# Feed-forward of a decoder layer: second h value in front of the chain of scales, and each half of h's turned codes waited for by itself

## The reference

```python
def bit_linear(x, w):            # activations: 8-bit codes per row, weights: -1, 0, 1
    qx = activation_quant(x)     # s = 127 / max(max|x|, 1e-5); clip(round(x * s), -128, 127) / s
    qw = weight_quant(w)         # s = 1 / mean|w|; clip(round(w * s), -1, 1) / s
    return qx @ qw.T

x = layernorm(x2)                                    # rows of 512
h = silu(bit_linear(x, w_gate)) * bit_linear(x, w_up)   # rows of 2048
h = ln_weight * (h * rsqrt(mean(h * h) + 1e-6))
y = x2 + bit_linear(h, w_down)                       # rows of 512
```

## Time and profile before

| | |
|---|---|
| runs | 803.2 us median of 3 (801.63 to 804.7) |
| profiled execution | 803.17 us, of which 801.3 us are the span from the first to the last instruction |
| PE busy over the span | 734.9 us (92%) |
| DVE busy | 595.3 us (74%) |
| ACT busy | 471.8 us (59%) |
| POOL busy | 332.9 us (42%) |
| feed-forward | first h at 603.4 us, last h at 783.0 us |
| mean granted clock of TensorE | 0.982 |

### The profile page before, as it was taken

The page is one execution under the profiler, slowest core; times in us unless marked ns, Lnnn a source line. Parts: engine busy times, 40 slices in busy tenths (PEclk is TensorE's granted clock), DMA queues, the critical chain, the costliest instruction groups (busy, mean ns, idle before and its releaser), DMA issues. The chain is left out here.

```text
span 801.3 us, 14101 instructions
## 1 busy us (share of the span) xinstructions
PE 734.9 (92%) x5113; PEld 507.1 (63%) x5130; DVE 595.3 (74%) x1102; ACT 471.8 (59%) x1024; POOL 332.9 (42%) x330
## 2 busy tenths in 40 slices
PE   6988999999999999999887879999978999999995
PEld 4766777777777777777654568888853443343442
DVE  6886766877668866676567557788857999999974
ACT  4555667666667665767545224444426676677663
POOL 2011214223042133534475154445525577677563
PEclk9999999999999999999989989999998999999999
DMA  9300021314032141305330175445221233343232
GB/s 314 107 1 28 27 85 49 106 40 146 28 106 70 64 151 35 106 28 187 104 106 1 53 284 199 172 184 211 92 63 60 52 93 93 80 102 82 61 71 66
DMA packets 55218, 78.33 MB, mean 98 GB/s; under 512 B 36335, under 2 KB 38383, under 8 KB 53424
## 3 DMA queue, kind: packets, MB, share of 16 engines
q1 hardware_dynamic: 46336, 51.99, 21.1%
q0 software_dynamic: 8528, 24.93, 9.0%
q10 hardware_dynamic: 288, 0.52, 0.2%
HBM read 56.92 MB, written 17.59 MB: 93 GB/s over the span
## 5 line engine op out<-in xcount | busy, mean ns | idle before, releaser
L557 ACT ACTIVATE probs<-s_ps,neg_max 128x512 f32<-128x512 f32 (+2 forms) x256 | 152.3, 610 | 19.2 <-DVE neg_max L726 17.7
L726 DVE TENSOR_REDUCE neg_max<-s_ps 128x2 f32<-128x1024 f32 (+2 forms) x128 | 124.6, 1015 | 34.2 <-PE s_ps L964 33.7
L984 PE MATMUL pT_ps<-ident,probs 128*128 128x128 f32 x832 | 114.8, 279 | 10.1 <-DVE probs L747 9.1
L569 ACT ACTIVATE probs<-pT_ps 128x512 f32<-128x512 f32 x96 | 57.4, 598 | 102.3 <-PE pT_ps L984 101.5
L984 PEld LDWEIGHTS pT_ps<-ident,probs 128*128 128x128 f32 x832 | 93.6, 143 | 25.2 <-DVE probs L747 11.7
L747 DVE COPY probs<-pT_ps 128x512 f32<-128x512 f32 x112 | 76.7, 684 | 36.8 <-PE pT_ps L984 36.0
L1669 POOL TENSOR_TENSOR xg_own<-h,ln_w_sb 128x512 f32<-128x512 f32 x64 | 83.2, 1309 | 39.6 <-DVE h L1757 35.1
L1848 PE MATMUL gate_ps<-w_tern,xqT_home 128*128 128x512 bf16 x252 | 67.6, 391 | 15.6 <-DVE h L1757 12.0
L897 PE MATMUL side_ps<-w_hi 128*128 128x512 f32 x172 | 71.0, 413 | 0.0
L420 POOL TENSOR_TENSOR aT_hi<-norm,one_col 128x512 fp32r<-128x512 f32 x15 | 15.6, 1040 | 125.9 <-DVE norm L738 87.7
L1848 PE MATMUL up_ps<-w_tern,xqT_home 128*128 128x512 bf16 x254 | 67.5, 388 | 0.1
(11 more groups left out here) (276 smaller groups left out, 1677.6 us busy)
## 6 DMA issues: line engine op xcount, KB each, us to landing
w_piece<-w_ffn SPq DMA_DIRECT2D x24, 512.0 KB
w_stage<-w_ffn SPq DMA_DIRECT2D x12, 1024.0 KB
xres<-x POOLq DMA_DIRECT2D x4, 1024.0 KB, 5.7
xn<-x SPq DMA_DIRECT2D x3, 1024.0 KB
x<-xres POOLq DMA_DIRECT2D x3, 1024.0 KB, 4.8
xn<-c SPq DMA_DIRECT2D x2, 1024.0 KB, 5.0
v_next<-c SPq DMA_DIRECT2D x2, 1024.0 KB, 8.0
xn<-x SPq DMA_DIRECT2D x4, 256.0 KB, 3.3
```

What stands on the lines that cost most here:

```text
L557: nc.scalar.activation(weights[qt][:, h, at:at + width(qt)], s_ps[:, h, 0:width(qt)], ACT.Exp, bias=neg_max[:, qt % 2, h:h + 1], accum_out ...
L569: nc.scalar.activation(out, turned_p, ACT.Identity).then_inc(slot_copied[0], 1)
L726: nc.vector.tensor_reduce(neg_max[:, qt % 2, 2 * s:2 * s + 2], s_ps[:, 2 * s:2 * s + 2, 0:width(qt)], AX.X, ALU.max, negate=True).then_inc ...
L984: last = nc.tensor.transpose(pT_ps[:, k % 2, h * P:h * P + P], weights[qt][:, h, a:z], ident[:])
```

## The change

Three edits.

1. `mean_of` computes the same product of `bn_mv`, -1 and `rstd` as a `tensor_scalar` with `rstd` as its pointer scalar, in place of a `scalar_tensor_tensor` with `rstd` as its second tensor.
2. On VectorE `hidden(t, 1)` moves from behind `quantize_h(t - 1)` to in front of `scale_x`, behind `top_of_x`.
3. `h_turned` becomes two semaphores, one for each half. `pack(t, n)` waits only for half n of tile t - 1, and `down(t, g)` only for half g // 2 of tile t.

```diff
     def mean_of(self, dve, t):
         i = t % 2
         dve.wait_ge(self.rstd_ready, t + 1)
-        self.nc.vector.scalar_tensor_tensor(self.mean_rstd[:, i:i + 1], self.bn_mv[:, i, 0:1], -1.0, self.rstd[:, i:i + 1],
-                                            ALU.mult, ALU.mult).then_inc(self.mean_ready, 1)
+        self.nc.vector.tensor_scalar(self.mean_rstd[:, i:i + 1], self.bn_mv[:, i, 0:1], self.rstd[:, i:i + 1], -1.0,
+                                     ALU.mult, ALU.mult).then_inc(self.mean_ready, 1)
...
-        hq_packed, h_turned = sem("hq_packed"), sem("h_turned")
+        hq_packed, h_turned = sem("hq_packed"), [sem("h_turned0"), sem("h_turned1")]
...
                         sp.dma_start_transpose(hqT[:, t % 2, n * FK // HALVES:(n + 1) * FK // HALVES, :],
-                                               hq[:, n * HALF:n * HALF + HALF]).then_inc(h_turned, 16)
+                                               hq[:, n * HALF:n * HALF + HALF]).then_inc(h_turned[n], 16)
...
                     if inside(t - 1):
-                        act.wait_ge(h_turned, t * HALVES * 16)
+                        act.wait_ge(h_turned[n], t * 16)
...
                     if inside(t + 2):
                         front.top_of_x(dve, t + 2)
+                    hidden(t, 1)
+                    if inside(t + 2):
                         front.scale_x(dve, t + 2)
                     if inside(t - 1):
                         scale_h(t - 1)
                         quantize_h(t - 1)
-                    hidden(t, 1)
                     hidden(t, 2)
...
-                        pe.wait_ge(h_turned, (t + 1) * HALVES * 16)
+                        pe.wait_ge(h_turned[g // HALVES], (t + 1) * 16)
```

## The result

| | before | changed |
|---|---|---|
| median | 803.11 us (801.63 to 804.7, 13 runs) | 809.19 us (806.01 to 812.71, 13 runs) |
| span of the profiled execution | 801.3 us | 808.3 us |

The ratio is 1.0076, with a 95% interval of 1.006 to 1.0092: slower by 6.1 us, where 6.0 were forecast.

The account below looks back on a forecast made before the run. The prediction took a loop over VectorE and ScalarE (11.81 us a round) as the bound, not PE. Steady rounds gain 0.45; +1.0+0.6+5.0-0.6 = +6.0 us on 803.2 gives 809.2 us, forecast's own range 805.5 to 812.

Parts of the forecast that it names:

- mean_of's step: On VectorE, mean_of in its new form no longer waits for GpSimd: 0.14 for 0.72 us, -0.58 a steady round.
- h(t,1) in the loop: On VectorE, h(t,1) between x_max and scale_x lengthens the round by 0.55 us, bounds 0.44 to 0.66.
- hold of the first hq_big: First hq_big of a pair waits on VectorE for GpSimd's weighted(t,1): 0.71 us remain, 0.50 held, bounds 0 and 0.71.
- the loop over VectorE and ScalarE: From hq_big through pack, gate_of, h(t,2), mean_of and maxima to the next hq_big: steps sum to the round, 11.81 us.
- The deciding term: h(t,1) early releases weighted(t,1) on GpSimd, which then runs into the first hq_big: +0.50 us a round.
- the row at 767.77: Profile row of hq_big starting 0.33 us before a GpSimd product ends; held 0.13, so remainder less 0.20.
- the rule of the Trainium skill: VectorE in two-port mode or with two SBUF inputs and GpSimd exclude each other for whole instructions: hold 0.71 us.
- Double rate: hq_big on VectorE runs at double rate: 1024 fp32 elements in 0.75 us, the maximum over as many half of 2.33.
- no meeting: Rival: the weighted product doesn't stand in hq_big's way, or holds it for 0.1 only; 803.2 us, chance 0.17.
- They lose nothing: Rounds 14 and 15 have no x; h(t,1) fits into VectorE's wait for h_rms; they win about 0.6 us together.
- Each half waited for by itself: Separate waits for the halves of h's turned codes: worth 0, since PE's slack just holds a common wait's 1.6 us.
- Nothing changes: Behind the last h, the end of the kernel stays as before: 0 us.

Follow-up runs that it names:

- second execution: The changed kernel, unchanged, run and profiled a second time to look at its last rounds again: 808.12 us.
- the version without the hold: Changed kernel, with one more GpSimd wait so weighted(t,1) starts only after both halves of tile t-1's codes are in hq_big: 802.78 us.
- Edit 1 with gate first: Kernel before with mean_of as tensor_scalar, and on ScalarE gate_of(t,2) in front of pack(t-1,0): 797.29 us, ratio 0.9928.

## Why the prediction was right

By its own steps, for the profiled executions:

| step | forecast | measured |
|---|---|---|
| mean_of's step | 0.72 to 0.14 | 0.72 to 0.12 |
| h(t,1) in the loop | +0.55 | 1.25 for 0.71: +0.54 |
| hold of the first hq_big | 0.71 us remain, 0.50 held | 0.74 remain, 0.54 held |
| xq_big | -0.03 | 0.48 for 0.50 |
| steady round | 12.26 us | 12.25 us |
| round 1 | +1.0 | +0.97 (0.48 from the first h to hq_big's start, 0.49 hold) |
| round 2 | +0.6 | +0.52 |
| rounds 3 to 13 | +5.0 | +4.9 |
| rounds 14 and 15 and the last hq_big | -0.6 | -0.6 |
| from the first h to the last hq_big | +6.0 | 185.12 to 190.91: +5.8 |
| in front of the first h | 0 | -0.5 |
| behind the last hq_big | 0 | +1.7 here, +0.05 in the second execution |

Each round is counted here with its own hold at its end, as in the forecast. So rounds 14 and 15, whose starts of hq_big in the table of experiments add up to the same 21.33 us in both kernels, are shorter by the 0.5 us that the hold of round 13 has already taken. They are so for the reason that was forecast: h(14,3) waits 0.92 us for f_gate and no longer 1.21 for up_ps, and y_of starts 0.66 to 0.67 us behind h(t,3) and no longer 0.77 to 0.80.

- *The bound.* Three kernels show the loop over VectorE and ScalarE, and not PE: edit 1 alone gains 7 us without touching PE, edit 3 alone removes a wait of PE and gains nothing, and gate_of in front of the pack takes 1.04 us off the round with the hold still in it.
- *The deciding term.* Keeping the product of h(t,1) from meeting hq_big brings back the 6 us with VectorE's order unchanged. That a double-rate tensor_scalar waits for a running GpSimd product is shown on hq_big (1.27 to 1.31 us) and on xq_big (1.06 us), that a small scalar_tensor_tensor over two SBUF tensors does on mean_of. The size followed the row at 767.77 (remainder less 0.20), not the whole remainder of the rule of the Trainium skill that the prediction quotes ("SBUF — State Buffer", section "Who interferes with whom"); the difference is 0.2 us a round. The records overlap here, so part of a hold may be hidden in an instruction's start, and the traces don't say more.
- *Double rate.* The comparison in the prediction (1024 elements in 0.75 us, where the maximum takes half of 2.33) gives a factor of 1.55 only. What speaks for the double rate is the growth: from 512 to 1024 columns a tensor_scalar grows by 0.27 us (xq_big 0.48, hq_big 0.75) and a maximum by 0.49 (x_max 0.68, hw_max 1.17).
- *Slips in the working.* The rival "no meeting" takes off 12 holds, but the sum has one in each of rounds 1 to 13: 13 holds of 0.5 bring 809.2 to 802.7 us, and the version without the hold took 802.78. By the same count the rule in the Trainium skill taken literally would cost 2.7 us more, not 2.5.
- *Not seen.* "They lose nothing" was right for rounds 14 and 15, though not because nothing is held there. The product of h(t,1) comes after the first hq_big, as forecast, and holds the second for 1.0 us. That this costs nothing is luck; the last section shows the rows.
- *Right in its time, wrong beside it.* "Each half waited for by itself ... worth 0 here" failed for rounds 14 and 15: it saves 2.07 us there, and 3.3 us in the medians. The forecast of the whole is untouched, because the -0.6 of these rounds was worked out with edit 3 in place. The statement that PE's wait would move to gate chunk 0 is half right (0.5 us); 0.9 us more of it are in front of y_ps, for y_of.
- *Behind the last h.* "Nothing changes" holds for the work; in the profiled execution PE waited 0.79 us for y_of, the clock was at 1.2 GHz for the next products, and four of them took 1.86 us for 1.02. In the second execution the same wait of 0.79 us came without a fall. Edit 1 with gate first, which leaves h(t,1) in its old place, has a fall too (0.68, in the down products of tile 14). So the fall isn't tied to the change by anything seen here. Whether it comes more often with it, as the wider spread of its runs (6.7 us for 3.1) may suggest, stays open.
- *Luck.* A median of 809.19 us for a forecast of 809.2 is closer than the working is. By the trace the change costs 5.8 us up to the last hq_big; what is in front of the first h (-0.5) and behind the last hq_big (+0.05 or +1.7) differs by execution, and the runs lie between 806.0 and 812.7.

## What to carry to other kernels

When a round's time equals a sum of steps that closes on itself over two engines, look at those steps first: here a wait of the busiest engine beside them cost nothing in the steady rounds. Before a producer is moved earlier, ask which instruction on another engine it releases and what will be running beside that one: here a 1.25 us GpSimd product slid under a double-rate VectorE instruction. An edit worth nothing alone was worth about 3 us once another one had changed what is late, so try them also in pairs.

## What the runs showed of the hardware

- A tensor_scalar of 128x1 with a pointer scalar isn't held by a GpSimd product (0.20 us in all rounds), the scalar_tensor_tensor of the same product is (0.80 us for 0.15).
- In rounds 14 and 15 of the changed kernel the product of h(t,0) runs when hq_big's first half starts, and that of h(t,1) is queued behind it on GpSimd. The second product gets in between the two halves: the first half takes 0.87 us, the second 1757 ns. VectorE, then GpSimd:

```profile
784.09 2.53 DVE L1794 TENSOR_SCALAR hq_big<-xg_own,h_mul 128x1024 f32<-128x1024 f32 x2
```

```profile
783.14 2.94 POOL L1669 TENSOR_TENSOR xg_own<-h,ln_w_sb 128x512 f32<-128x512 f32 x2
```

That took 1.0 us of VectorE and nothing of the round: the held half ends at 784.09+2.53 = 786.62, and ScalarE, busy with gate_of(t,2) until 786.70, starts the second pack at 786.66. Round 15 is 10.50 us, as in the kernel with the products kept apart.
